# Folding the softmax sums to 64 rows before the matmul with ones, in an attention layer

## The reference

```python
xr = x.reshape(B, C, S).transpose(0, 2, 1)
qkv = (xr @ w_qkv + b_qkv).reshape(B, S, N_HEADS, 3 * d_k)     # 8 heads of 64
q, k, v = jnp.split(qkv, 3, axis=-1)
attn = jnp.einsum('bihd,bjhd->bijh', q, k) * scale
attn = jax.nn.softmax(attn, axis=2)
out = jnp.einsum('bijh,bjhd->bihd', attn, v).reshape(B, S, N_HEADS * d_k)
out = out @ w_proj + b_proj
return out.transpose(0, 2, 1).reshape(B, C, H, W) + x
```

## Time and profile before

| | |
|---|---|
| time, median of 3 runs | 4060.68 us (4059.18 to 4065.95) |
| the profiled execution, its own time | 4065.14 us |
| its span, first to last instruction | 4063.4 us |
| granted TensorE clock, mean | 0.993 of full speed |
| PE busy | 97% of the span, 18464 matmuls |
| DVE, ACT, POOL busy | 80%, 72%, 76% |
| DMA | 453 MB, mean 112 GB/s |

### The profile page before, as it was taken

One profiled execution on the slowest core, in us unless ns is written; L12 is line 12 of the kernel. 1 busy time (PEld: TensorE's weight loads), 2 busy tenths in 40 slices (PEclk: granted clock), 3 DMA queues, 4 the chain that ended last, 5 costly groups with the idle time before them and its releaser, 6 DMA issues.

```text
span 4063.4 us, 60262 instructions
## 1 busy us (share of the span) xinstructions
PE 3937.5 (97%) x18464; PEld 3361.4 (83%) x18464; DVE 3249.1 (80%) x4382; ACT 2931.4 (72%) x5527; POOL 3074.6 (76%) x2436
## 2 busy tenths in 40 slices
PE   4999999999999999999999999999999999999997
PEld 3878888888888888888888888888888888888885
DVE  3888878888888888888888888887888888888884
ACT  2777777777777777777777777777777777777774
POOL 1787787787777877787777777877778777877775
PEclk9999999999999999999999999999999999999998
DMA  6343443444334344434434434443443444344331
GB/s 184 83 122 105 111 114 99 119 115 130 101 97 123 105 124 117 112 105 101 130 104 118 115 102 109 122 126 97 106 116 103 125 118 110 105 103 128 104 94 61
DMA packets 263376, 453.33 MB, mean 112 GB/s; under 512 B 107920, under 2 KB 118160, under 8 KB 258960
## 3 DMA queue, kind: packets, MB, share of 16 engines
q1 hardware_dynamic: 263056, 449.48, 41.4%
HBM read 206.58 MB, written 41.42 MB: 61 GB/s over the span
## 4 chain that ended last, share of the span: by engine, by line
PE 83%; POOL 7%; ACT 3%; issue 3%; DVE 2%; DMA 1%; SPq 1%; ACTq 0%; POOLq 0%; DVEq 0%
PE ps_g L390 22%; PE s L412 10%; PE ps_o L524 10%; PE ps_o L522 10%; PE st L465 10%; PE st L463 10%; PE ps_g L406 9%; POOL p_hl L746 4%; POOL x_l L730 2%; ACT p_hl L586 1%; PE st L509 1%; PE st L510 1%; DVE acc L647 1%; ACT p L583 1%; POOL o L753 1%
## 5 line engine op out<-in xcount | busy, mean ns | idle before, releaser
L746 POOL TENSOR_TENSOR p_hl<-p,p_hl 128x512 fp32r<-128x512 f32 x2048 | 2605.7, 1296 | 912.0 <-ACT p_hl L586 911.1
L583 ACT ACTIVATE p<-st 128x512 f32<-128x512 f32 x2048 | 1230.7, 601 | 716.6 <-PE st L465 686.9
L650 DVE TENSOR_REDUCE nm<-s 128x1 fp32r<-128x1024 f32 x1024 | 1252.0, 1223 | 417.1 <-PE s L412 406.3
L647 DVE TENSOR_TENSOR acc<-acc,p 128x512 f32<-128x512 f32 x1792 | 1237.1, 690 | 29.4 <-ACT p_hl L586 0.8
L586 ACT ACTIVATE p_hl<-st 128x512 fp32r<-128x512 f32 x2048 | 1236.7, 604 | 0.0
L522 PE MATMUL ps_o<-p_hl,v_hl 128*128 128x512 f32 x2048 | 803.5, 392 | 5.0 <-POOL p_hl L746 4.3
L465 PE MATMUL st<-q,k 128*128 128x512 f32 x2048 | 804.5, 393 | 0.0
L524 PE MATMUL ps_o<-p_hl,v_hl 128*128 128x512 f32 x2048 | 802.0, 392 | 0.0
L463 PE MATMUL st<-q,k 128*128 128x512 f32 x2048 | 800.0, 391 | 0.5 <-DMA q<-max_d 0.3
L390 PE MATMUL ps_g<-x_h,wq 128*128 128x512 f32 x2016 | 711.8, 393 | 31.6 <-POOL x_l L730 31.6
L412 PE MATMUL s<-k,q 128*128 128x512 f32 x2048 | 647.0, 397 | 11.5 <-DVE nm L650 8.5
(11 more groups left out here) (79 smaller groups left out, 3673.9 us busy)
## 6 DMA issues: line engine op xcount, KB each, us to landing
wq<-wq_d SPq DMA_DIRECT2D x128, 512.0 KB, 5.0
k<-qk_h SPq DMA_DIRECT2D x256, 256.0 KB, 4.3
wv<-wv_d SPq DMA_DIRECT2D x32, 1024.0 KB, 5.1
q<-qk_h SPq DMA_DIRECT2D x128, 256.0 KB, 3.8
q<-qk_l SPq DMA_DIRECT2D x128, 256.0 KB, 4.9
k<-qk_l SPq DMA_DIRECT2D x128, 256.0 KB, 5.2
q<-q SPq DMA_DIRECT2D x256, 128.0 KB, 4.0
rinv<-rinv_d SPq DMA_DIRECT2D x256, 128.0 KB, 2.8
```

Of the source, the lines that this page charges most:

```text
L583: nc.scalar.activation(p[:, to, :], st[slot % RING][:], ACT.Exp)
L647: nc.vector.tensor_tensor(acc[:], acc[:], probs, ALU.add).then_inc(acc_done, 1)
L650: nc.vector.tensor_reduce(nm[:, it:it + 1], s1[:], AXX, ALU.max, negate=True).then_inc(max_done, 1)
L746: nc.gpsimd.tensor_tensor(p_l[:, to, :], p[:, to, :], p_h[:, to, :].bitcast(f32), ALU.subtract).then_inc(pl_done, 1)
```

## The change

The sum over the 128 key rows gets a step ahead of it. ScalarE copies rows 64 to 127 of `acc` to `fold` (in U % 4 == 0, in the place of the rounding to `acc_h`), VectorE adds rows 0 to 63 to it (U % 4 == 1, in the place of `acc_l`). In the same unit, **between its two probability tiles**, ScalarE rounds `fold` into rows 0 to 63 of `fold_hl`, and GpSimd, also between its two tiles, writes the rest into rows 64 to 127. One matmul with ones sums all 128 rows of `fold_hl`, so both parts at once; it stands one unit later, in U % 4 == 2. The copy of the row of sums and its store move one unit later with it, the load back to the start of U % 4 == 0, the reciprocal from the end of U % 4 == 0 to U % 4 == 1, ahead of the group's last step; SP's store and load of `rinv` stay in U % 4 == 1 and 2.

```diff
@@ slot, sum_slot
-            sums = (unit + 2) // 4
+            sums = (unit + 1) // 4
-            return 0 if self.drain else self.slot(4 * half + 5, 1) + 1
+            return 0 if self.drain else self.slot(4 * half + 6, 1) + 1
@@ buffers
-        acc_h = sb("acc_h", [P, HALF], f32r)
-        acc_l = sb("acc_l", [P, HALF], f32r)
+        fold = sb("fold", [D, HALF])
+        fold_hl = sb("fold_hl", [P, HALF], f32r)
@@ sync
+                    if U % 4 == 0 and B.on(half := (U - 8) // 4, HALVES):
+                        n = half % 2
+                        sp.wait_ge(row_stored[n], at(16 * HEADS, 16 * (half // 2 + 1)))
+                        sp.dma_start(s64[n][:], sum_d[n].rearrange("(p c) -> p c", p=D)).then_inc(s64_loaded[n], 16)
                     if u == 0 and B.now:
...
-                    if U % 4 == 2 and B.on(half := (U - 6) // 4, HALVES):
+                    if U % 4 == 3 and B.on(half := (U - 7) // 4, HALVES):
                         n = half % 2
                         sp.wait_ge(st_free, at(SLOTS, B.sum_slot(half) + 1))
                         sp.dma_start(sum_d[n:n + 1, :], sum_row[32 * n:32 * n + 1, :]).then_inc(row_stored[n], 16)
-                    if U % 4 == 3 and B.on(half := (U - 7) // 4, HALVES):
...
@@ tensor
-                    if U % 4 == 1 and B.on(half := (U - 5) // 4, HALVES):
+                    if U % 4 == 2 and B.on(half := (U - 6) // 4, HALVES):
                         slot = B.sum_slot(half)
                         pe.wait_ge(st_free, at(SLOTS, slot - 2))
-                        pe.wait_ge(accl_done, at(HALVES, half + 1))
-                        nc.tensor.matmul(st[slot % RING][:], ones[:], acc_h[:], start=True, stop=False)
-                        nc.tensor.matmul(st[slot % RING][:], ones[:], acc_l[:], start=False, stop=True
+                        pe.wait_ge(foldl_done, at(HALVES, half + 1))
+                        nc.tensor.matmul(st[slot % RING][:], ones[:], fold_hl[:], start=True, stop=True
                                          ).then_inc(st_done, 1)
@@ scalar
+                        if e == 0 and U % 4 == 1 and B.on(half := (U - 5) // 4, HALVES):
+                            act.wait_ge(fold_done, at(HALVES, half + 1))
+                            nc.scalar.copy(fold_hl[0:D, :], fold[:]).then_inc(foldh_done, 1)
...
-                        nc.scalar.copy(acc_h[:], acc[:]).then_inc(acch_done, 1)
-                    if U % 4 == 1 and B.on(half := (U - 5) // 4, HALVES):
+                        if (v := at(HALVES, half)) is not None:
+                            act.wait_ge(foldl_done, v)
+                        nc.scalar.copy(fold[:], acc[D:P, :]).then_inc(fold_copied, 1)
+                    if U % 4 == 2 and B.on(half := (U - 6) // 4, HALVES):
@@ vector
-                        dve.wait_ge(acch_done, at(HALVES, half + 1))
-                        nc.vector.tensor_tensor(acc_l[:], acc[:], acc_h[:].bitcast(f32), ALU.subtract
-                                                ).then_inc(accl_done, 1)
+                        dve.wait_ge(fold_copied, at(HALVES, half + 1))
+                        nc.vector.tensor_tensor(fold[:], acc[0:D, :], fold[:], ALU.add).then_inc(fold_done, 1)
...
-                    if U % 4 == 0 and B.on(half := (U - 8) // 4, HALVES):
+                    if U % 4 == 1 and B.on(half := (U - 9) // 4, HALVES):
                         n = half % 2
                         dve.wait_ge(s64_loaded[n], at(16 * HEADS, 16 * (half // 2 + 1)))
                         nc.vector.reciprocal(r64[n][:], s64[n][:]).then_inc(recip_done, 1)
@@ gpsimd, between the two tiles of a unit
+                        if e == 0 and U % 4 == 1 and B.on(half := (U - 5) // 4, HALVES):
+                            if B.now:
+                                pool.wait_ge(pl_done, at(2 * UNITS, 2 * U + 1))
+                            pool.wait_ge(foldh_done, at(HALVES, half + 1))
+                            nc.gpsimd.tensor_tensor(fold_hl[D:P, :], fold[:], fold_hl[0:D, :].bitcast(f32),
+                                                    ALU.subtract).then_inc(foldl_done, 1)
+                            pool.wait_ge(foldl_done, at(HALVES, half + 1))
```

More of the change, by code:

```diff
@@ L195, in attention_kernel @@
         acc_done = sem("acc_done")
-        acch_done = sem("acch_done")
-        accl_done = sem("accl_done")
+        fold_copied = sem("fold_copied")
+        fold_done = sem("fold_done")
+        foldh_done = sem("foldh_done")
+        foldl_done = sem("foldl_done")
         row_stored = [sem(f"row_stored{i}") for i in range(NH)]
@@ L349, in body @@
                         sp.dma_start(sum_d[n:n + 1, :], sum_row[32 * n:32 * n + 1, :]).then_inc(row_stored[n], 16)
-                    if U % 4 == 3 and B.on(half := (U - 7) // 4, HALVES):
-                        n = half % 2
-                        sp.wait_ge(row_stored[n], at(16 * HEADS, 16 * (half // 2 + 1)))
-                        sp.dma_start(s64[n][:], sum_d[n].rearrange("(p c) -> p c", p=D)).then_inc(s64_loaded[n], 16)
                     if U % 4 == 1 and B.on(half := (U - 9) // 4, HALVES):
@@ L575, in body @@
                         nc.scalar.copy(tmp[rows, half % 2, :], ps_o[other, :]).then_inc(half_moved, 1)
-                    if B.now:
-                        for e in range(2):
+                    for e in range(2):
+                        if B.now:
                             slot, to = B.slot(U, e), U % 2 * 2 + e
@@ L642, in add_probs @@
                     if (v := B.at(HALVES, unit // 4)) is not None:
-                        dve.wait_ge(accl_done, v)
+                        dve.wait_ge(fold_done, v)
                     nc.vector.tensor_copy(acc[:], probs).then_inc(acc_done, 1)
```

## The result

| | before | after |
|---|---|---|
| time, median of 5 runs | 4060.68 us (4058.99 to 4065.95) | 4135.05 us (4130.77 to 4138.87) |
| ratio, 95% interval | | 1.0181 [1.0167, 1.0195] |
| the profiled execution / its span | 4065.14 / 4063.4 us | 4133.67 / 4131.9 us |
| granted TensorE clock, mean | 0.993 | 0.989 |

What follows compares the result with a forecast made beforehand. PE bounds ordinary units, GpSimd is as full in units 45 to 51 and 1 to 5. Fourteen entries at +2.57 give +36, the first and last +2 each: +40 on 4060.7, about 4100 us; range 4056 to 4122.

Steps and rivals of the forecast that it cites:

- +2.61: Units 45 to 52, each entry: two folds of 1.43 less 0.25 us idle GpSimd time delay PE's group of unit 52.
- +1.35: Units 1 to 6, each entry: folds in units 1 and 5 delay PE's PV matmuls by 1.35 us.
- The taken 1.43: GpSimd's price for each half's fold in us: 1.30 for the operation, the rest lost overlap and waits.
- by rows: Rival: GpSimd's fold on 64 rows costs 0.78 us, so 4061 us, no change; chance 0.13.
- the rival of free releases: Rival: releases of `ps_g` cost nothing, only GpSimd does; +1.24 us for each entry, 4080 us; chance 0.11.
- the even pairs: Even heads, U = 9, 25, 41, 53, 57: `stage` frees the bank early enough, so each gains 0.227 us.
- the odd pairs: Odd heads, U = 13, 17, 29, 61: PE waits for `qk_l` behind the reciprocal; each changes by only -0.03 us.
- +0.27: U = 21: ScalarE's later `qk_h` delays `qk_l`, PE waits 0.50 us for the bank; +0.27 us each entry.
- it would grow to 5 us: PE's wait for `x_l` in each entry was to grow from about 2.2 us to 5 us.
- +2 us for each: First and last batch entry: units without a group, where GpSimd sets the pace, were to cost 2 us in each.
- costed at nothing: Moved DMAs: SP's later row store, load back and maxima were to cost 0 with the median landing of 2.2 us.
- SP's queue late: Rival: late stores of reciprocals hold up maxima and moves of q and k; 4120 us; chance 0.10.

Runs made afterwards that it cites:

- experiment 1: GpSimd's fold operation taken out of the kernel after: 4062.48 us; a like 64x512 operation on constants put alone into the kernel before: 4142.5 us.
- Experiment 2: Matmuls on constants ahead of PE's wait for `x_l` in unit 52: 14 in the kernel after, 4111.88 us; nine in the kernel before, 4054.34 us.
- the fold in its easy places: Kernel after, only eleven halves folded, behind the units' own steps, reciprocal in U % 4 == 0, nine constant matmuls: 4037.24 us; kernel before with nine: 4054.34.
- the last kernel of experiment 4: Kernel after with eleven halves folded, five by two ones matmuls, reciprocal back in U % 4 == 0, no constant matmuls: 4054.68 us, ratio 0.9986.

## Why the prediction went as it did

**Right: where it hurts, and the sign.** GpSimd has no spare time in units 45 to 52 and 1 to 6, so the fold is paid there: +2.61 forecast and +2.60 measured, +1.35 and +1.51. GpSimd around the fold of unit 45:

```profile
2009.26 1.29 POOL L751 TENSOR_TENSOR p_hl<-p,p_hl 128x512 fp32r<-128x512 f32 x1 [0.42 <-ACT p_hl L587]
2010.63 1.29 POOL L758 TENSOR_TENSOR fold_hl<-fold,fold_hl 64x512 fp32r<-64x512 f32 x1
2012.00 1.29 POOL L751 TENSOR_TENSOR p_hl<-p,p_hl 128x512 fp32r<-128x512 f32 x1
```

From the first tile to the fold 1.37 us and from the fold to the second tile 1.37 us, where two `p_l` in a row start 1.25 us apart: one fold adds 1.49 us here. The taken 1.43 is 0.06 too little, and twice that is most of the missing 0.16 in units 1 to 6. In units 45 to 52 two such folds less 0.25 make 2.73, and the median is +2.69; that the mean meets 2.61 to 0.01 is luck. That 64 rows take no less than 128 was the decisive choice between two bounds, and it came from another engine, VectorE, of which nothing showed that GpSimd would be like it; it came out right. The rival "by rows" falls with 1290 ns (its 4061 leaves out the 4 us of the first and the last entry that the sum has; with them it is 4064, and the rival of free releases is 4082). The Trainium skill's "GPSIMD Engine Reference", section "Instruction dispatch", says that all eight cores receive each instruction, every one for its own 16 partitions, and that it is complete when all are done. By that rule 64 rows take as long as 128; the trace agrees, 1290 against 1296 ns.

**Right: the even pairs.** They gain 0.23 us each, down from 4.12 + 3.67 to 3.67 + 3.89.

**Nearly right: the odd pairs; unit 22 by other terms.** The odd pairs gain nothing, forecast 0.03. Units 13 and 14 of after, against the earlier trace rows:

```profile
1885.46 0.39 PE L465 MATMUL st<-q,k 128*128 128x512 f32 x1
...
1889.76 0.18 DVE L713 RECIPROCAL r<-s 64x8 f32<-64x8 f32 x1
1889.87 0.69 DVE L634 SCALAR_TENSOR_TENSOR qk_l<-ps_g,bqk,qk_h 128x512 fp32r<-128x512 f32 x1
1890.62 0.73 PE L392 MATMUL ps_g<-os_hl,wp_h 128*128 128x512 f32 x2
...
1893.24 0.39 PE L465 MATMUL st<-q,k 128*128 128x512 f32 x1
```

From 1885.46 to 1893.24 are 7.78 us, before 7.78 too. The group starts right behind `qk_l`, as forecast, 0.06 us after its end. Two terms were off and nearly cancel: `qk_l` starts 0.11 us after the reciprocal (0.15 taken; moving it back gave 0.05 to 0.07), and PE, once stopped, takes some 0.11 us more for its first matmul: two of the group are listed with 0.73 us together, those of the kernel before come 0.23 apart. Unit 22 came out at +0.37 for +0.27, but not by its terms. The group starts 0.19 us earlier than forecast, and what takes that back, besides the 0.11, is a wait that the prediction did not have: units 18 to 21 carry `os_l`, so GpSimd is full there too, and PE's third PV matmul of unit 22 waits for its second tile:

```profile
1922.01 1.29 POOL L751 TENSOR_TENSOR p_hl<-p,p_hl 128x512 fp32r<-128x512 f32 x1
...
1923.07 0.39 PE L525 MATMUL ps_o<-p_hl,v_hl 128*128 128x512 f32 x1
1923.35 0.50 PE L523 MATMUL ps_o<-p_hl,v_hl 128*128 128x512 f32 x1
1923.69 0.40 PE L525 MATMUL ps_o<-p_hl,v_hl 128*128 128x512 f32 x1
```

The starts are 0.28 and 0.34 us apart in place of 0.23, 0.16 us in all. That GpSimd's operation does this is shown by experiment 1: put alone into the kernel before, it costs 0.36 us in unit 22.

**Wrong: the clock was a term of nothing.** The sum let PE resume from a wait at full pace. The earlier trace rows gave the length of that wait, the prediction said that it would grow to 5 us, and left it there; the trace of before already showed matmuls of some 0.63 us behind this wait in 4 of 15 entries, 27 in all, where that of after shows 98. The wait itself grew to 3.5 us, not 5 (52.8 us in 15), because PE already waits some 1.1 us for keys in unit 50. Experiment 2 puts the clock at 14 to 17 us of the change's 74. This is the largest part of the miss.

**Wrong: the first and the last entry.** "+2 us for each" is +6.4 and +6.1. No row was laid under that. In units without a group PE is not the bound, GpSimd is, and there a fold costs its whole self. Unit 53 of the last entry:

```profile
4040.56 1.29 POOL L751 TENSOR_TENSOR p_hl<-p,p_hl 128x512 fp32r<-128x512 f32 x1 [0.51 <-ACT p_hl L587]
4041.93 1.28 POOL L758 TENSOR_TENSOR fold_hl<-fold,fold_hl 64x512 fp32r<-64x512 f32 x1
...
4044.63 0.51 PE L523 MATMUL ps_o<-p_hl,v_hl 128*128 128x512 f32 x1 [0.33 <-POOL p_hl L751]
```

Units 54, 58 and 62 of that entry are 1.36, 1.35 and 1.49 us longer, and 1.47, 1.44 and 1.47 with the operation alone added to the kernel before. The first entry has such a unit at 46 (+1.38; +0.30 without the operation). Its units 18 (+1.35) and 42 (+1.61) are longer for another reason, moved keys that come late:

```profile
151.84 0.39 PE L467 MATMUL st<-q,k 128*128 128x512 f32 x1
153.29 0.85 PE L414 MATMUL s<-k,q 128*128 128x512 f32 x2 [1.06 <-DMA k<-qk_l]
```

They stay at +1.49 and +1.72 without GpSimd's operation and fall to +0.26 and +0.40 with the reciprocal moved back: the store of the reciprocals, which waits for them, stands ahead of the moves in SP's order. So some 2.3 us of the first entry's 6.4 belong to the DMAs, which the prediction costed at nothing.

**Nearly right: the DMAs, costed at nothing.** PE does wait for keys now (19.7 us, 18 times). In 15 entries that wait is in unit 50, ahead of the wait of unit 52 that is later anyway, where it costs nothing more; in units 18 and 42 of the first entry it costs the time given above. The rival "SP's queue late" gave 4120 with late maxima and late moves: no unit is longer by a wait for maxima, late moves there are, but at some 2 us and not 20. What the cover hid is the load back: 27 us, when it comes a few steps later.

**The sum, closed.** On the span: forecast +40. To it come the clock, 15 us in the middle entries (14 x 1.07); the edge entries, 4.4 + 4.1 us; small terms, some 6.5 us (57.5 - 36 - 15); less 1.5 us up to the first unit: 68.5 us. The medians add 6: the profiled execution of before lies 4.5 us above its median, that of after 1.4 below. This is scatter of single executions and says nothing of the change. The clock alone is more than the 13 us by which the range was missed: its upper end was a rival of its own at 4122, and there was no case for what a longer wait does to the matmuls behind it.

## What to carry to other kernels

An engine with 24% of idle time may have none in the stretch that counts: cost an added operation unit by unit, at its full price where the engine has no gap, and move it only into units that have one. A wait that grows on TensorE is costed by its length and, besides, by the matmuls behind it at 1.2 GHz; look whether the trace of before already shows matmuls at double spacing behind it. Where the wait can't be avoided, matmuls on constants in it can be worth as much as the change: 23 us in the kernel after, against 17 us for the fold in its easy places.

## What the runs showed of the hardware

- After a wait of 3.75 us the granted clock was 0.50 for 5 us. After waits of 1.8 to 2.5 us it fell in some entries and not in others: 4 of 15 before, 7 of 14 in the last kernel of experiment 4. The Trainium skill's "TensorE: Matmul & The Clock Gate", section "What's actually happening", has the gate set by how busy the engine has been, with throttled as its default. The trace agrees: with the wait filled the clock was 1.00 in the same stretch.
- A 64x512 operation of GpSimd took 1290 ns, a 128x512 one 1296; on ScalarE the copies of 64x512 took 586 and 612 ns, one of 128x512 589.
- A wait for the operation just ahead costs: two GpSimd operations in a row start 1.25 us apart, one that waits for the other 1.37.
- TensorE's first matmul behind a stop takes 0.30 to 0.34 us to the next, in place of 0.23, at full clock (2112.77 to 2113.07 us and 1923.35 to 1923.69 us in the kernel after).
